# An LSTM's recurrent matmuls ordered gate group by gate group

## What is computed

```python
# x (32, 64, 256), h0 (32, 256), Wx and Wh (256, 1024), b (1024)
xW = jnp.einsum('ntd,dg->ntg', x, Wx) + b
def step(carry, xw_t):
    prev_h, prev_c = carry
    a = xw_t + prev_h @ Wh
    i, f, o = (jax.nn.sigmoid(a[:, k * Hd:(k + 1) * Hd]) for k in range(3))
    g = jnp.tanh(a[:, 3 * Hd:])
    next_c = f * prev_c + i * g
    next_h = o * jnp.tanh(next_c)
    return (next_h, next_c), next_h
...
# for the rows h of all 64 steps
h = s0 * (concat([h, -h]) @ k0pm);  h = 2 * relu(h)      # 256 -> 1024
h = s1 * (h @ k1pm);                h = 2 * relu(h)      # 1024 -> 1024
return x + s2 * (h @ k2pm)                               # 1024 -> 256
```

## Time and profile before

| | us |
|---|---|
| median of 3 runs | 280.08 (279.79 to 280.56) |
| the profiled execution, whole time | 279.52 |
| its span, from first to last instruction | 277.7 |
| TensorE (PE) busy in it | 273.4 |
| VectorE (DVE) busy | 203.2 |
| ScalarE (ACT) busy | 157.8 |

### The profile page before, as it was taken

How to read it: one execution, slowest core, us unless ns; L and a number is a source line. 1 busy time by engine, 2 the same in 40 slices (tenths; PEclk the granted TensorE clock), 3 DMA queues, 4 the chain that set the end, 5 groups by cost and what they waited for, 6 DMA issues and landing times.

```text
span 277.7 us, 8789 instructions
## 1 busy us (share of the span) xinstructions
PE 273.4 (98%) x3616; PEld 223.8 (81%) x3616; DVE 203.2 (73%) x750; ACT 157.8 (57%) x481; POOL 2.0 (1%) x10
## 2 busy tenths in 40 slices
PE   8999999999999999999999999999999999999996
PEld 5888777778999998999999998999999995544553
DVE  3877888878888888888888888888887876431103
ACT  4797787878565656555556565555665545311100
POOL 0100000000000000000000000000000000000000
PEclk9999999999999999999999999999999999999999
DMA  6970000000000000000000000000000100010002
GB/s 186 384 306 1 4 2 0 2 4 2 2 2 0 5 21 21 2 2 4 21 20 5 1 30 13 2 2 22 22 2 0 40 4 2 0 38 2 0 0 76
DMA packets 4791, 8.72 MB, mean 31 GB/s; under 512 B 656, under 2 KB 2704, under 8 KB 4624
## 3 DMA queue, kind: packets, MB, share of 16 engines
q1 hardware_dynamic: 4464, 7.64, 7.8%
q10 hardware_dynamic: 288, 0.52, 0.6%
HBM read 6.07 MB, written 2.10 MB: 29 GB/s over the span
## 4 chain that ended last, share of the span: by engine, by line
PE 93%; ACT 3%; DVE 2%; issue 0%; DVEq 0%; POOL 0%; POOLq 0%
PE WK L437 50%; PE WK L420 11%; PE G L401 10%; PE ACC L453 9%; PE G L392 9%; PE G L476 1%; PE G L420 1%; ACT tT L580 1%; PE ACC L420 1%; ACT xw L518 1%; PE G L453 1%; ACT tC L585 0%; DVE aT L730 0%; DVE uT L739 0%; DVE cD L741 0%
## 5 line engine op out<-in xcount | busy, mean ns | idle before, releaser
L437 PE MATMUL WK<-h,k 128*128 128x256 f16 (+1 forms) x992 | 125.6, 276 | 0.4 <-DVE h L750 0.4
L437 PEld LDWEIGHTS WK<-h,k 128*128 128x128 fp8e5 x992 | 93.6, 98 | 15.1 <-issue 2.6
L580 ACT ACTIVATE tT<-aT 128x128 f32<-128x128 f32 x126 | 39.0, 310 | 58.1 <-DVE aT L730 56.8
L627 DVE SCALAR_TENSOR_TENSOR h<-WK,h 128x256 f16<-128x256 f32 (+1 forms) x105 | 42.6, 440 | 25.0 <-ACT h L544 25.0
L730 DVE TENSOR_REDUCE aT<-G 128x128 f32<-128x256 f32 x128 | 48.1, 418 | 7.7 <-PE G L401 7.1
L544 ACT ACTIVATE h<-WK 128x256 f16<-128x256 f32 (+1 forms) x104 | 36.2, 387 | 28.8 <-PE WK L437 28.8
L526 ACT ACTIVATE G<-xw 128x256 f32<-128x256 f32 x126 | 46.6, 370 | 0.0
L420 PE MATMUL WK<-xs,wxs 128*128 128x512 f32 x168 | 43.5, 402 | 0.0
L401 PE MATMUL G<-h,w 128*128 128x64 f16 x1008 | 39.5, 192 | 0.0
L392 PEld LDWEIGHTS G<-h,w 128*128 128x128 f16 x1008 | 32.9, 96 | 5.8 <-DVE h L747 4.1
L392 PE MATMUL G<-h,w 128*128 128x32 f16 x1008 | 35.1, 176 | 0.1
(11 more groups left out here) (66 smaller groups left out, 133.1 us busy)
## 6 DMA issues: line engine op xcount, KB each, us to landing
out_y<-x SPq DMA_DIRECT2D x14, 128.0 KB, 1.8
x<-in_x SPq DMA_DIRECT2D x3, 512.0 KB, 8.5
xw<-in_wh SPq DMA_DIRECT2D x4, 256.0 KB, 6.0
k<-in_k SPq DMA_DIRECT2D x1, 1024.0 KB, 10.5
xw<-in_wx SPq DMA_DIRECT2D x3, 256.0 KB, 6.1
x<-in_x ACTq DMA_DIRECT2D x2, 256.0 KB, 3.6
k<-in_k SPq DMA_DIRECT2D x1, 512.0 KB, 7.9
xw<-in_wx SPq DMA_DIRECT2D x2, 128.0 KB, 3.2
```

The costliest lines, as they stand in the source:

```text
L437: ins = eng.matmul(layer_src(tile), w, rhs, start=a == 0, stop=last)
L580: eng.activation(tT[:, B * j0:B * j1], aT[:, j0:j1].rearrange("p j b -> p (j b)"), ACT.Tanh, scale=half_gain0 if t == 0 else half_gain).th ...
L627: eng.scalar_tensor_tensor(layer_dst(tile, 1), layer_src(tile), 0.0, layer_dst(tile, 0), ALU.max, ALU.subtract).then_inc(lo_made[tile[0]])
```

## The change

The order of a step's matmuls. Before: 8 of line 392 into G0, 8 of line 392 into G1, the wait for h's low part, 8 of line 401 into G0 (then `gates[0]`), 8 of line 401 into G1 (then `gates[1]`). After: 8 of line 392 into G0, the wait for h's low part, 8 of line 401 into G0 (then `gates[0]`), 8 of line 392 into G1, 8 of line 401 into G1 (then `gates[1]`). No matmul is added or taken away, and the plan of the fill stays as it is. `e` drops a wait that it has already made, so the second pass of the loop issues no second wait for `hl_made`.

```diff
                 for g, (j0, j1) in enumerate(GROUPS):
                     e.wait_ge(seeded[g], t + 1)
                     for j in range(j0, j1):
                         e.wait_ge(wlo, j // 2 + 1)
                         for k in range(2):
                             eng.matmul(G[g][:, 64 * (j - j0):64 * (j - j0) + B], w16[:, 1, j, k], hi[:, k],
                                        start=False, stop=False, skip_group_check=True)
-                if t > 0:
-                    e.wait_ge(hl_made, t)
-                else:
-                    e.wait_ge(hz_lo, 1)
-                for g, (j0, j1) in enumerate(GROUPS):
+                    if t > 0:
+                        e.wait_ge(hl_made, t)
+                    else:
+                        e.wait_ge(hz_lo, 1)
                     for j in range(j0, j1):
                         for k in range(2):
                             ins = eng.matmul(G[g][:, 64 * (j - j0):64 * (j - j0 + 1)], w16[:, 0, j, k],
```

## The result

The changed kernel takes 280.60 us (median of 22 runs, 280.11 to 281.14) against 280.24 us (22 runs, 279.79 to 280.91) of the kernel before; the ratio is 1.0016, with a 95% interval from 1.0009 to 1.0022. That is +0.45 us (0.25 to 0.62): a small loss, within the 0.3% that the forecast called "same". The two medians lie 0.36 us apart. 280.8 us was forecast, +0.70 us.

The account below looks back on a forecast made before the run. TensorE, busy 273.4 of 277.7 us, was taken as the bound. +0.80 (steps 8 to 63), 0.00 (early steps) and -0.10 (end) sum to +0.70 us on 280.08, forecasting 280.8 us, range 279.8 to 282.2.

Parts of the forecast that it names:

- The wait that moves: TensorE's wait for `hl_made`: costs nothing before; after, below 0.25 us between line 747's end and line 392, TensorE stops.
- lead: Time from line 747's end to the first matmul of line 392; forecast to grow by 0.10 us.
- What the chain gains: VectorE's adds after the matmuls: second add starts 1.07 us after the step's start, not 1.18; h comes 0.10 earlier.
- The sum over steps 8 to 63: TensorE's stops in eleven steps cost 1.04 us, waits saved give back 0.24: net +0.80 us.
- The early steps and the end: Steps 2 to 7 taken as zero (-0.2 to +0.2); TensorE's wait after step 63 gives back 0.10 us.
- rival 1: TensorE's wake-up in mid-stream is dearer, 0.15 us; gives 282.4 us; chance 0.13.
- rival 2: TensorE's stops are swallowed where a wait for h follows; gives 280.0 us; chance 0.11.
- Rival 3: Earlier first group wins if no stop is left: -0.8, some 0.5 in steps 4 to 7; 279.2 us; chance 0.05.
- rival 4: TensorE's clock falls in stopped stretches, eleven steps at twice their length; gives 316 us; chance 0.01.

Follow-up runs that it names:

- e5_four_ahead: Changed kernel with only four short matmuls ahead of the wait for h's low part: 282.22 us against 279.90 for the kernel before, ratio 1.0086.
- e2_twelve_ahead: Changed kernel with twelve short matmuls, not eight, ahead of the wait for h's low part: 279.67 us against 279.79 for the kernel before, ratio 0.9992.
- e6_one_wait: Changed order with the wait for h's low part ahead of all matmuls, high part's wait removed: 285.66 us against 279.90 for the kernel before.
- e3_late_gate: Changed kernel with `gates[0]` raised later, by the last of group 1's short matmuls: 282.25 us against 279.79 for the kernel before, ratio 1.0096.
- e1_no_stop: Changed order, but line 400 uses h's high part in both halves, never the low part: 279.24 us against 279.79 for the kernel before.
- e4_none_ahead: Changed order with the wait for h's low part added ahead of all 32 matmuls: 286.51 us against 279.79 for the kernel before, ratio 1.0239.

## Why the prediction was right, point by point

**The wait that moves.** Right in place and form. The stops begin at the lead forecast: step 19 (0.24) stops for 0.01, step 15 (0.24) for 0.01, and no step with a lead over 0.25 stops. In each stopped step the first long matmul begins 0.056 us after the end of the instruction that makes h's low part, which is also what the starts of held steps show without rounding: the 0.05 of the prediction. e5_four_ahead, e2_twelve_ahead and e6_one_wait move the threshold to 0.35, 0.15 and 0.45 us, and their times follow within 0.3 us.

**What the chain gains.** Right: where VectorE is free the second add starts at 1.07, and in 40 of the steps 8 to 63 the lead grows by 0.09 to 0.11. It grows by up to 0.20 in steps behind one that was stopped or late, and by less in the steps that had waited. Taking the gain away costs some 2 us (e3_late_gate), leaving the stops away while it stays brings 0.5 to 0.6 below before (e1_no_stop). One sentence was wrong: that the first add does not move where VectorE is still emptying a tile. In step 26 it moved from 1.14 to 1.05 after the step's start, since VectorE began its emptying earlier against TensorE. The sum did not follow that sentence: it took the full 0.10 for step 27, whose lead did grow from 0.08 to 0.17.

**The sum over steps 8 to 63.** Forecast: stops of 1.04 us in eleven steps, 0.24 of waits saved, +0.80. Measured between the starts of these steps: 12 stops, 0.88 us; waits saved 0.28 (0.13 of it in step 45); restarts 0.13 more. A resumed stream loses 0.013 (step 28 above), and nine of the twelve steps have a restart more than before: seven had none, and steps 12 and 45 now resume twice. The forecast counted six restarts in its 1.04, so 1.04 stands against 1.01. The distance from step 8 to step 63 grew by 0.73 in one pair of profiles and 0.72 in the other. The twelfth stop is that of step 15, whose old lead of 0.147 fell just outside the prediction's cut; it stops for 0.01. The one stop clearly mis-sized is that of step 28, 0.10 instead of 0.14: step 27 had stopped as well, which made TensorE later against the chain, and the sum had treated the steps as independent.

**The early steps and the end.** Taken as zero and -0.10. Steps 0 to 8 grew by 0.03 and 0.00 in the two pairs of profiles, with four stops of 0.08 to 0.18 in steps 4 to 7 swallowed as said. The wait after step 63 shrank by 0.09.

**The rivals.** The wake-up in mid-stream costs 0.056, not 0.15 (rival 1). The stops are swallowed only in steps 4 to 7 (rival 2). Rival 3 named the gain if no stop were left, -0.8; e1_no_stop made that case and gave 0.5 to 0.6, so its mechanism is real and its condition isn't met; its term for steps 4 to 7 was too large, 0.5 against 0.21. The granted clock stayed at full from the first step to the last in every profile (rival 4). The spacing that this rival read from the earlier trace rows as 0.225 us is (3.60 - 0.42) / 15 = 0.21, since one of those matmuls takes 0.42. The rule of the Trainium skill, "TensorE: Matmul & The Clock Gate", section "A second HAM failure mode: psum-queue depth-cycling", that frequent short idles between groups can bring the slower clock, finds no support here, with up to 25 stops in e3_late_gate at the full granted clock.

**The size.** The trace's own account is +0.65 us, the forecast +0.70, the medians +0.36 and +0.55. The sum was thus right to 0.05 by the trace, while +0.70 lies above the interval of the runs (0.25 to 0.62). The scatter of the start, of which no step of the prediction spoke, can account for that, but it is argued from four profiles. That 280.8 came within 0.2 us of the measured 280.60 is partly luck: the median of three runs it started from, 280.08, was 0.16 below that of 22 runs, and this made up for half of the 0.34 us by which +0.70 exceeds the medians' +0.36.

## What to carry to other kernels

When a wait is moved forward past covering work, ask for each step how far the consumer comes behind the producer, not how much idle time the profile reports: the cost is the sum of what is missing in each, and only the steps under the threshold pay. Work moved away from in front of a consumer should stop where the next resource takes over as the limit: here the second add was bound by its own matmuls after four of the eight were moved, and the other four bought nothing but the stops. On a chain that runs beside a full engine, a shorter chain is worth only the waits and stops that it removes or shortens: 0.5 to 0.6 us in e1_no_stop, some 2 us where the stops were there to be shortened (e3_late_gate against the changed kernel).

## What the runs showed that was not expected

A wait costs 0.05 us more when it is not the weight load itself that waits but an instruction of its own in front of it: 0.10 us from the end of the VectorE instruction to the matmul (e4_none_ahead, 59 steps), against 0.056 (e6_one_wait, 40 steps). That is about 0.9 us over the kernel by the medians. In these kernels it was the wait written first that the weight load carried, `hh_made` in e4_none_ahead and `hl_made` in e6_one_wait. By this the wait that ends last should be written first; e4_none_ahead with its two waits in the other order would test that, and was not run. Nor was a third wait as such ruled out: e4_none_ahead has three in front of its first matmul, the other kernels two. The 0.15 us at the end of the recurrence has such an instruction for `hl_made` in front of it too, the last of the kernel before, at 231.4 us; there it began only 0.04 us after line 750's end.
